# Halves for the loads of x and the stores of the context, other places for L1, the gates and the scans

## The reference, cut to what matters

```
x = x + L0(x)   # h = gelu(x fc1^T + b), 2048 wide; out = h [fc2 | expert]^T + b, 512 wide
x = x + L1(x)   # x W[subject]^T + b
x = x + L2(x)   # ctx  = causal_ema(x, tau_ctx)
                # wg   = sigmoid([x, ctx] Wg^T + bg);  gated = x * wg
                # mod  = 0.5 + sigmoid(gelu(x Wn1^T + bn1) Wn2^T + bn2)       4 values a token
                # temporal = sum_d softmax(blend)_d * causal_ema(gated * mod_d, tau_d)
                # gate = sigmoid(temporal Wtemp^T + btemp);  soma = gelu(x Wsoma^T + bsoma)
                # out  = layernorm((soma * gate) Wout^T)
x = x + L3(x)   # x W[category] + b
```

## Time and profile before

| | |
|---|---|
| median of three runs | 1328.61 us |
| profiled execution | 1330.79 us, span 1329.1 us |
| mean granted clock of TensorE | 0.988 |
| TensorE busy | 1283.3 us (97%), 6109 matmuls |
| VectorE busy | 1060.9 us (80%) |
| ScalarE busy | 721.9 us (54%) |
| moved by DMA | 262.62 MB, mean 198 GB/s |
| chain that ended last | TensorE 81%, VectorE 9%, DMA 5%, ScalarE 3% |

### The profile page before, as it was taken

One profiled execution on the slowest core, in us unless ns is written; L12 is line 12 of the kernel. 1 busy time (PEld: TensorE's weight loads), 2 busy tenths in 40 slices (PEclk: granted clock), 3 DMA queues, 4 the chain that ended last, 5 costly groups with the idle time before them and its releaser, 6 DMA issues.

```text
span 1329.1 us, 17485 instructions
## 1 busy us (share of the span) xinstructions
PE 1283.3 (97%) x6109; PEld 1072.7 (81%) x6109; DVE 1060.9 (80%) x1698; ACT 721.9 (54%) x1369; POOL 80.9 (6%) x102
## 2 busy tenths in 40 slices
PE   8999899999999999999999989699999999999998
PEld 7788688888888887778887868678888888888877
DVE  7877677787786887667874698989898989898974
ACT  6577455775565775366863333353535353636354
POOL 0010000000000000000000000002200220031000
PEclk9999899999999999989999999799999999999999
DMA  8257643648655667535569668674557454754301
GB/s 286 96 173 234 211 152 127 214 145 274 197 169 159 214 221 229 181 125 180 187 232 323 211 242 323 253 290 162 211 176 283 180 210 183 266 186 178 141 17 64
DMA packets 110830, 262.62 MB, mean 198 GB/s; under 512 B 9960, under 2 KB 32488, under 8 KB 102552
## 3 DMA queue, kind: packets, MB, share of 16 engines
q1 hardware_dynamic: 90592, 180.12, 39.5%
q10 hardware_dynamic: 15320, 65.60, 13.9%
q0 software_dynamic: 4832, 15.79, 3.1%
HBM read 181.19 MB, written 80.28 MB: 197 GB/s over the span
## 4 chain that ended last, share of the span: by engine, by line
PE 81%; DVE 9%; DMA 5%; issue 3%; ACT 3%; ACTq 0%; DVEq 0%; SPq 0%
PE bank L1544 27%; PE bank L1545 26%; PE bank L1546 26%; DMA hb_in<-hb_dram 2%; DMA mod_t<-mod_dram 1%; DVE h_hl L2010 1%; DVE w_hl L2010 1%; DVE drive L2247 1%; DVE x_lo L2010 1%; DVE temporal L2260 1%; DVE x_raw L2162 1%; DMA mod_dram<-mod_row 1%; DVE soma L2310 1%; DMA x_slot<-x2hl_dram 0%; DVE t_lo L2010 0%
## 5 line engine op out<-in xcount | busy, mean ns | idle before, releaser
L1544 PE MATMUL bank<-h_hl,w_hl 128*128 128x512 f32 x512 | 203.1, 397 | 19.6 <-DVE w_hl L2010 18.8
L1546 PE MATMUL bank<-h_hl,w_hl 128*128 128x512 f32 x512 | 201.7, 394 | 0.0
L1545 PE MATMUL bank<-h_hl,w_hl 128*128 128x512 f32 x512 | 201.6, 394 | 0.0
L1544 PE MATMUL bank<-t_hi,sp_hl 128*128 128x512 f32 x448 | 175.4, 392 | 3.9 <-DVE t_lo L2010 1.4
L1545 PE MATMUL bank<-t_lo,sp_hl 128*128 128x512 f32 x448 | 174.4, 389 | 0.0
L1546 PE MATMUL bank<-t_hi,sp_hl 128*128 128x512 f32 x448 | 174.4, 389 | 0.0
L1544 PEld LDWEIGHTS bank<-h_hl,w_hl 128*128 128x128 f32 x512 | 97.5, 190 | 44.4 <-DVE h_hl L2010 23.0
L1546 PEld LDWEIGHTS bank<-h_hl,w_hl 128*128 128x128 f32 x512 | 97.5, 190 | 20.8
L1545 PEld LDWEIGHTS bank<-h_hl,w_hl 128*128 128x128 f32 x512 | 97.7, 191 | 19.8
L1544 PEld LDWEIGHTS bank<-t_hi,sp_hl 128*128 128x128 f32 x448 | 84.2, 188 | 24.7 <-issue 2.4
L1546 PEld LDWEIGHTS bank<-t_hi,sp_hl 128*128 128x128 f32 x448 | 84.1, 188 | 17.6
(11 more groups left out here) (232 smaller groups left out, 3084.5 us busy)
## 6 DMA issues: line engine op xcount, KB each, us to landing
wg_hl<-wg_dram ACTq DMA_DIRECT2D x26, 1536.0 KB, 7.5
fc_raw<-in_fc_w SPq DMA_DIRECT2D x32, 512.0 KB, 4.1
hb_dram<-hb_out SPq DMA_DIRECT2D x64, 256.0 KB, 2.3
hb_in<-hb_dram ACTq DMA_DIRECT2D x64, 256.0 KB, 3.4
x2hl_dram<-x_hl POOLq DMA_DIRECT2D x28, 512.0 KB, 5.4
x_slot<-x2hl_dram SPq DMA_DIRECT2D x26, 512.0 KB, 5.2
wg_hl<-wg_dram SPq DMA_DIRECT2D x6, 1536.0 KB, 9.2
stage<-in_l_w SPq DMA_DIRECT2D x32, 256.0 KB, 3.3
```

The costliest lines, as they stand in the source:

```text
L1544: eng.matmul(ps, w_hi, x_hi, start=first, stop=False, skip_group_check=resumed)
L1545: eng.matmul(ps, w_hi, x_lo, start=False, stop=False, skip_group_check=resumed)
L1546: return eng.matmul(ps, w_lo, x_hi, start=False, stop=final, skip_group_check=resumed)
```

## The change

- `load_x`, `store_ctx` and `load_xt` move a half (two chunks of 512 KB together) and are called twice; waits on their semaphores count 16 * HALVES.
- In the pairs 1 and 2 the first half of the context store of the tile before goes to unit 7. The second tile's x goes in halves at uses 4 and 9, each after SyncE has waited for that use, instead of in one piece at use 10.
- `parked_units`: pair 0 has K8+2, +5, +8, +10, +13 instead of K8+1, +3, +5, +7, +8, +13; pair 1 has unit 4 more.
- SyncE's list for the last pair's second tile is paced anew by `uses_done`.
- L1 of tile 6 comes after uses 2 to 5 (before: 3, 4, 6, 7), the gates of tile 0 after 4, 7, 9, 11 (before: 4, 8, 11, 14). The orders of ScalarE and VectorE follow, up to the gates of tile 1.
- `wg_tanh` issues the load of the gate weights ahead of the tanh, from gate 7 on; SyncE loads gate 6's.
- From tile 2 on, the second tanh of te stands before two copies of x3, and spikes 1 before `x3_low`.

```diff
-        parked_units = ((4, 5, 6, 7, K8 + 1, K8 + 3, K8 + 5, K8 + 7, K8 + 8, K8 + 13),
-                        (1, 2, 3, 5, 6, 7, K8 + 3, K8 + 6, K8 + 8, K8 + 13),
+        parked_units = ((4, 5, 6, 7, K8 + 2, K8 + 5, K8 + 8, K8 + 10, K8 + 13),
+                        (1, 2, 3, 4, 5, 6, 7, K8 + 3, K8 + 6, K8 + 8, K8 + 13),
...
-            def load_x(t):
+            def load_x(t, h):
                 if t >= 2:
-                    on.wait_ge(s_ctxst, 16 * (t - 1))
+                    on.wait_ge(s_ctxst, 16 * HALVES * (t - 1))
...
-                eng.dma_start(x_raw[t % 2][:, :, :], x[t]).then_inc(s_xld[t % 2], 16)
+                half = slice(HALF * h, HALF * (h + 1))
+                eng.dma_start(x_raw[t % 2][:, half, :], x[t, :, half, :]).then_inc(s_xld[t % 2], 16)
...
+            def store_ctx(t, h):
+                half = slice(HALF * h, HALF * (h + 1))
+                on.wait_ge(s_ctxlo, KC * t + HALF * (h + 1))
+                eng.dma_start(ctx_dram[t, :, half, :], x_raw[t % 2][:, half, :]).then_inc(s_ctxst, 16)
...
                     if p and k == 7:
-                        load_x(HALVES * p)
+                        load_x(HALVES * p, 0)
+                        load_x(HALVES * p, 1)
+                        store_ctx(HALVES * p - 1, 0)
...
-                if p:
-                    store_ctx(HALVES * p - 1)
+                if 0 < p < PAIRS - 1:
+                    store_ctx(HALVES * p - 1, 1)
...
                     pass_staged(p, K8 + j)
-                    if p and j == 10:
-                        load_x(HALVES * p + 1)
+                    if p and j in (4, 9):
+                        on.wait_ge(s_fc2, 2 * HC * p + HC + j)
+                        load_x(HALVES * p + 1, int(j == 9))
...
             uses_done(1)
-            load_xt(0)
+            load_xt(0, 0)
             pass_staged(PAIRS - 1, K8 + 2)
             uses_done(2)
+            load_xt(0, 1)
+            uses_done(3)
+            store_ctx(LAST - 2, 1)
+            uses_done(4)
             load_wg(1)
-            uses_done(4)
-            load_x(LAST)
+            uses_done(5)
+            load_wsoma(0)
             uses_done(6)
             load_wg(2)
+            uses_done(7)
+            load_x(LAST, 0)
+            uses_done(8)
+            store_x2(LAST - 1)
             uses_done(9)
-            store_x2(LAST - 1)
-            load_wsoma(0)
+            load_wg(3)
+            uses_done(10)
+            load_x(LAST, 1)
+            uses_done(11)
             load_wsoma(1)
-            uses_done(11)
-            load_wg(3)
             uses_done(12)
             load_wsoma(2)
             load_wsoma(3)
-            store_ctx(LAST - 1)
+            uses_done(13)
             load_wg(4)
+            store_ctx(LAST - 1, 0)
+            store_ctx(LAST - 1, 1)
...
             load_wg(5)
+            load_wg(6)
             store_x2(LAST)
...
             def wg_tanh(i, m):
                 ps = wg_bank(i, m)
+                g = KC * i + m + 2
+                if 7 <= g < KC * NT:
+                    on.wait_ge(s_pe["WG"], g - 1)
+                    eng.dma_start(wg_hl[g % 2][:, :, :, :].bitcast(F32), wg_dram[g % KC]).then_inc(s_wg[g % 2], 16)
                 on.wait_ge(s_g, KC * i + m + 1)
                 eng.activation(ps[:, :], ps[:, :], ACT.Tanh, bias=bg_sb[:, m:m + 1], scale=0.5
                                ).then_inc(s_wgt, 1)
-                g = KC * i + m + 2
-                if 6 <= g < KC * NT:
...
@@ ScalarE, last pair, second tile
-                    if j in (7, 11, 14):
-                        q_of(0, (7, 11, 14).index(j))
-                    if j == 8:
+                    if j in (7, 10, 12):
+                        q_of(0, (7, 10, 12).index(j))
+                    if j == 7:
                         wg_tanh(0, 0)
-                    if j == 12:
+                    if j == 11:
                         wg_tanh(0, 1)
...
@@ ScalarE, loop
                 te_tanh(r - 1, 0)
-                for m in range(KC):
+                for m in range(HALVES):
                     x3_hi_of(r - 2, m)
-                for m in range(1, KC):
-                    te_tanh(r - 1, m)
+                te_tanh(r - 1, 1)
+                for m in range(HALVES, KC):
+                    x3_hi_of(r - 2, m)
+                te_tanh(r - 1, 2)
+                te_tanh(r - 1, 3)
...
@@ TensorE
-                        l1(LAST - 1, 0)
-                    if j == 4:
-                        l1(LAST - 1, 1)
-                    if j in (6, 7):
-                        l1(LAST - 1, j - 4)
-                    if j in (4, 8, 11, 14):
-                        gate(0, (4, 8, 11, 14).index(j))
+                    if j in (2, 3, 4, 5):
+                        l1(LAST - 1, j - 2)
+                    if j in (4, 7, 9, 11):
+                        gate(0, (4, 7, 9, 11).index(j))
...
-                for m in range(KC):
+                for m in range(SH):
                     te(r - 1, m)
-                gate(r, 1)
+                if r == 1:
+                    gate(r, 1)
+                te(r - 1, SH)
+                if r > 1:
+                    gate(r, 1)
...
@@ VectorE, last pair, second tile
+                    if j in (5, 6, 7, 8):
+                        x2_of(t, j - 5)
                     if j == 7:
                         gate_sum(0, 0)
+                        traces_a(0, 0)
                     if j == 8:
-                        traces_a(0, 0)
+                        traces_b(0, 0)
+                    if j == 9:
+                        x2_lo(t, 0)
+                        x2_lo(t, 1)
+                        traces_c(0, 0)
                     if j == 10:
-                        traces_b(0, 0)
-                    if j == 11:
-                        traces_c(0, 0)
+                        x2_lo(t, 2)
+                        x2_lo(t, 3)
                         traces_d(0, 0)
                         gate_sum(0, 1)
+                    if j == 11:
+                        traces_a(0, 1)
+                        traces_b(0, 1)
                     if j == 12:
-                        context(LAST - 1, 0)
-                        context(LAST - 1, 1)
-                        traces_a(0, 1)
-                    if j == 13:
-                        context(LAST - 1, 2)
-                        context(LAST - 1, 3)
-                        traces_b(0, 1)
-                    if j == 14:
-                        context_lo(LAST - 1, 0)
-                        context_lo(LAST - 1, 1)
                         traces_c(0, 1)
                         gate_sum(0, 2)
+                        context(t, 0)
+                        context(t, 1)
+                    if j == 14:
+                        traces_d(0, 1)
+                        context(t, 2)
+                        context(t, 3)
...
@@ VectorE, loop
                 spikes(r - 1, 0)
+                spikes(r - 1, 1)
                 x3_low(r - 2, 0, 2)
                 x3_low(r - 2, 2, 2)
+                spikes(r - 1, 2)
                 traces_b(r, 0)
-                spikes(r - 1, 1)
-                spikes(r - 1, 2)
```

More of the change, by code:

```diff
@@ L697, in load_xt @@
                 on.wait_ge(s_x2st, 16 * (NT if i >= 2 else i + 1))
-                eng.dma_start(xt[i % 3][:, :, :], x2_dram[i]).then_inc(s_xt[i % 3], 16)
+                half = slice(HALF * h, HALF * (h + 1))
+                eng.dma_start(xt[i % 3][:, half, :], x2_dram[i, :, half, :]).then_inc(s_xt[i % 3], 16)
             def load_slot(i, c):
@@ L864, in _ @@
             load_slot(2, 1)
-            store_ctx(LAST)
-            load_xt(2)
+            store_ctx(LAST, 0)
+            store_ctx(LAST, 1)
+            load_xt(2, 0)
+            load_xt(2, 1)
             load_l3w(0)
@@ L1435, in _ @@
                 x2_hi(LAST, c)
-            for m in range(KC):
+            for m in range(SH):
                 te_tanh(0, m)
-            for m in range(KC):
-                spikes_hi(0, m)
             q_of(1, 1)
             wg_tanh(1, 1)
+            te_tanh(0, 3)
+            for m in range(SH):
+                spikes_hi(0, m)
+            q_of(1, 2)
+            spikes_hi(0, 3)
             ctx_hi(LAST, 0)
             ctx_hi(LAST, 1)
-            q_of(1, 2)
             wg_tanh(1, 2)
@@ L2574, in _ @@
             traces_a(1, 0)
+            spikes(0, 0)
             for c in range(KC):
                 x2_lo(LAST, c)
-            for m in range(SH):
-                spikes(0, m)
-            traces_b(1, 0)
+            spikes(0, 1)
+            context(LAST, 0)
+            context(LAST, 1)
+            spikes(0, 2)
+            gate_sum(1, 1)
+            context(LAST, 2)
             spikes(0, 3)
-            traces_c(1, 0)
             spikes_low(0, 0, 2)
             spikes_low(0, 2, 2)
-            context(LAST, 0)
-            context(LAST, 1)
-            traces_d(1, 0)
-            gate_sum(1, 1)
-            traces_a(1, 1)
+            traces_b(1, 0)
+            gate_sum(1, 2)
```

(13 more changed lines are left out.)

66 lines of the change are left out of this document (34 added, 32 removed).

## The result

The changed kernel takes 1299.40 us (median of 4 runs, 1298.98 to 1299.45) against 1328.78 for the kernel before (4 runs beside it, 1326.76 to 1329.28): a ratio of 0.978, interval 0.976 to 0.980. That is 29.4 us less. The forecast was 1303.4, 4.0 us above. The profiled execution of the changed kernel took 1299.40, the one of before 1330.79: 31.4 us apart, also in their spans.

The account below looks back on a forecast made before the run. TensorE bounds the kernel (1283.3 of 1329.1 us busy), leaving idle time and half clock to win. Terms -7.3 - 5.9 - 1.9 + 0.8 - 7.8 - 3.1 = -25.2 us take 1330.79 to 1305.6, less 2.2 for the median: 1303.4; range 1294 to 1313.

Parts of the forecast that it names:

- Pair 0: Near 142 us: other units for the parked blocks remove ScalarE's wait for a store and its half clock, -7.3 us.
- Pair 2, end: At 562 us: x in halves at uses 4 and 9 leaves a 1.3 us wait without half clock, -5.9 us.
- Pair 2, start: At 514 us: half the context store moved to unit 7 lands `hb` 1.7 us earlier, -1.9 us.
- The price in the burst of unit 7: 0.52 MB more ahead of the first `hb` load costs +0.8 us at pair 1 and +1.5 at pair 3.
- Rival 3: Queues alternate, pair 2's loads waited for something else, so -5.9 and -1.9 fail: 1311.2 us, chance 0.07.
- The halves themselves: Fixed cost near 2 us per transfer would be in no sum; in series, 20 more transfers would cost 40 us.
- Last pair: Second tile, first layer: reordered L1 and gates remove 7.2 of TensorE's 8.0 us of waits and half clock.
- The sum of gate 3: Last pair, tile 0: VectorE reaches it at 789.0 in place of 795.1, 6.1 us; TensorE then waits 2.3 at `so_pair`.
- To te(1, 0): Whole last-pair part up to te(1, 0), with VectorE idle 9.5 us: -9.3 us, -7.8 with the later start.
- TensorE alone comes to the same: Before te(1, 0): gate(1, 3) wait shrinks from 11.8 to 4 to 7 us, keeping half clock; te at 883.8.
- Loop: Tiles 2 to 7: spikes 1 ahead of `x3_low`, ready 5 us early, removes short TensorE waits, -3.1 us.
- Rival 1: Last pair less tight: VectorE idles 3 us, not 9.5, and late starts cost nothing: 1294.6 us, chance 0.16.

Follow-up runs that it names:

- run 1: Kernel before with only the units of the parked blocks in pairs 0 and 1 changed: 1321.64 us against 1329.13.
- run 3: Kernel before with every load of x made as two 512 KB transfers issued at once, not paced: 1330.48 us, ratio 1.0012.
- run 4: Changed kernel with the half context store taken out of unit 7, both halves going where the whole store went before: 1301.24 us.
- run 10: Changed kernel with sum of squares sooner, tile 1's gate 3 sum later, chunk 0's scans and first step sooner, tile 2's slot loads held until gate(1, 2): 1296.56 us.
- run 6: Changed kernel with tile 0's sum of squares moved ahead of the first two trace steps of tile 1's chunk 2 in VectorE's list: 1299.36 us.
- run 5: Changed kernel with only the loop's order of scans, spikes and tanhs put back in tiles 2 to 7: 1304.38 us.
- run 8: Changed kernel with sum of squares sooner, slot loads held until gate(1, 1), te(0, 3) ahead of gate(1, 1), and VectorE's idle time partly filled: 1299.54 us.
- run 11: Kernel of run 10 with tile 0's gate 3 sum and the last tile's four additions of x ahead of chunk 2's scans: 1293.91 us.
- run 12: Kernel of run 11 with the last tile's four split x2 stores also held until gate(1, 2) is done: 1296.70 us.
- run 9: Kernel of run 8 with the sum of gate 3 of tile 1 moved behind the first two trace steps of chunk 1: 1298.95 us.

## Why the prediction was right, and where it was not

The time lies 4.0 us below the forecast, the sum 6.2 us short (31.4 measured, 25.2 forecast). The other 2.2 go the other way, and that is luck: I took the profiled execution's distance to its median (2.2 us) for both kernels, and the changed kernel's profiled execution is its median.

- **Pair 0.** Forecast -7.3, measured -7.8 in the trace and -7.5 in run 1. Right, mechanism and size.
- **Pair 2, end.** Forecast a wait of 1.3 us left without half clock, -5.9; measured 1.24 us, -6.1. Run 3 shows that halves without the spacing do not do it.
- **Pair 2, start.** -1.9 forecast, -2.7 measured, -1.8 to -2.8 over the nine traces with this code. The size is right; the reason is not, since run 4, which moves no half, has the same start of pair 2 within that scatter: two transfers, with the load issued between them, are enough.
- **The price in the burst of unit 7.** Forecast +0.8 and +1.5; measured -0.6 at pair 1 and -0.5 at pair 3, so this is the step that failed, 3.4 us in all. It took the earlier trace rows ("it waits for what was issued before it") for a rule of every burst. In the changed kernel SyncE's store of a parked block issued at 679.34 took 15.1 us and the `hb` load issued at 680.63 took 6.3:

```profile
l3w_dram<-stage_hi SPq DMA_DIRECT2D x1, 256.0 KB, 15.1
hb_in<-hb_dram ACTq DMA_DIRECT2D x1, 256.0 KB, 6.3
```

  The load on the other queue landed ahead of most of SyncE's backlog. Rival 3 thus had a part of the truth. The packets by queue (packets, MB, share of the 16 engines; q1 is SyncE's queue, q10 ScalarE's) show what the issue times don't. In the kernel before, in 554.9:558.9 (from the issue of the `hb` load on) and in 559:562:

```profile
q1 hardware_dynamic: 172, 0.77, 78.7%
...
q1 hardware_dynamic: 236, 0.76, 66.1%
q10 hardware_dynamic: 164, 0.31, 26.7%
```

  In the changed kernel, in 680.7:684 and in 684.1:686.9:

```profile
q1 hardware_dynamic: 255, 1.36, 99.1%
...
q1 hardware_dynamic: 269, 0.87, 77.8%
q10 hardware_dynamic: 145, 0.26, 24.6%
```

  Both loads moved nothing for 3.5 to 4.1 us and then went beside SyncE's packets, at 0.10 and 0.09 MB a microsecond. The one at 680 had landed by 686.9; the one at 554.85 met a store of GpSimd's, issued 2.3 us behind it, that moved 0.63 MB from 562 to 564.6 while ScalarE's queue moved 0.15. In all 14 traces, a load on ScalarE's queue with none of its own under way moved its first packet between 0.95 us (queues empty) and 5.3 us after its issue, 3.5 where SyncE's transfers went on landing for 14 us more. So neither "it waits for all that was issued before it" nor "SyncE's transfers don't matter" holds: a load pays a start of up to 5.3 us and then a shared rate. The rule of the Trainium skill ("DMA: Bandwidth & Descriptors", section "Queues, rings and completion order"), packets in turn from each queue, fits the second part in both cases and not the first. What sets the start was not settled.
- **The halves themselves.** No fixed cost of 2 us each is in any sum: run 3 makes eight more transfers than before and is 0.1% slower. The Trainium skill ("DMA: Bandwidth & Descriptors") gives the 2 us in its section "Anatomy of one DMA — SWDGE (gpsimd) path", for transfers that GpSimd issues, and not under "Bandwidth", where the prediction placed it.
- **Last pair.** Uses 12 to 15: 7.2 of 8.0 forecast, 8.7 measured in all (from -17.7 to -26.4 in the table), with what each wait adds. The sum of gate 3: 6.1 us sooner forecast, 6.6 measured (ends at 770.8, before at 795.1, less 17.7 us). `so_pair`: 2.3 and 2.0.
- **To te(1, 0).** Forecast 9.3 us less, measured 10.0 from the start of pair 3. VectorE idles 8.6 us of the 94.4 between the sum of gate 3 and te(1, 0), forecast 9.5 (the five terms that the prediction lists for it add up to 8.8; the slip of 0.7 is not in the forecast, which took TensorE's 883.8):

```profile
771.00:865.40 94.40, 85.69 (x429) 71.59 (x428) 85.83 (x115) 40.80 (x71) 0.00 (x0) 0.93 0.80 301
```

  The parts are less good than the sum, whose closeness is in part luck. The load for gate(1, 3) was forecast at 14 us from its issue and took 10.0: too much was laid on SyncE's backlog again, and run 10 shows that a megabyte less gives nothing. The wait was 3.1 in place of 4 to 7. On the other side the 3.6 us before `ss` brought a second stretch of half clock, which was in no sum: the 25 matmuls from `ss` on take 9.07 us, in run 6 without it 6.12. TensorE then reached te(1, 0) 2.0 us after VectorE's low half was ready (863.45 and 865.46). "TensorE alone comes to the same" was nearly so: run 6 takes 6.6 us off TensorE there and gains 1.9.
- **Loop.** -3.1 forecast, -4.4 measured: the mechanism is right (run 5), the size left out 0.23 us for each of five waits (1.1) and the 0.4 us of a sixth, of 0.13 us, in the tile from te(1, 0) to te(2, 0), less 0.2 for the wait for `y_sb`, which grew. VectorE's idle time, given as 3.4 us a tile, was 5.1 to 6.4 in the kernel before; that changes nothing.
- **Rival 1** (waits less tight, late starts cost nothing) gave 1294.6 and is the one the errors lean to: the starts did cost nothing, VectorE's idle time is the forecast's.

## What to carry to other kernels

Price a stall as its idle time, plus what the restart costs (0.23 us here, 0.16 of it lost overlap), plus the half clock that may follow it, and look whether a wait of 3 us that you leave standing will bring that clock. Where two engines reach the same point within 2 us of each other, a wait taken from the one alone is worth what the other leaves; runs 6 and 8 gained nothing in the median; run 11, which also reorders the in-order list of the later engine so that it idles 5.5 us between 771 and te(1, 0) in place of 8.6, gained 5.5 us. A transfer held back must be followed to its last reader before it is held.

## What the hardware showed unexpectedly

- A load on ScalarE's queue moved its first packet up to 5.3 us after its issue where SyncE's queue was busy (0.95 with empty queues, 3.4 to 3.5 with 14 to 17 us of SyncE's transfers still to land in the changed kernel), and went beside SyncE's packets from then on; it landed ahead of a backlog issued sooner (6.3 us beside 15.1, 10.0 beside 17.6), but took 9.8 to 10.1 us with 1 MB of x just ahead and a store of GpSimd's behind.
- The 1536 KB load took 9.9 to 10.0 us while the queues moved 408 to 417 GB/s in all (811 to 821 us, run 10 and the changed kernel), and 7.9 us in run 12, where the last of SyncE's transfers landed 1.2 us after its issue.
- Half clock (1.2 GHz) followed or went with every TensorE wait of 2.6 us or more between 30 and 1290 us in the traces of this case (from 2.61 to 11.95 us), and none of 1.7 us or less. Of the waits between 1.75 and 2.2 us four had it (1.81, 1.95 and twice 2.00, in runs 4, 5 and 9) and the others, up to 2.17 us, had not.
